# Row statistics, index casts and a weight load redistributed in the opening of a graph-convolution and expert kernel

## What is computed

```python
xn = layernorm(x)                                   # eps 1e-5
h  = ln_w * xn * rsqrt(mean(xn**2) + 1e-6)          # per row
out = h @ W_root + bias                             # 1024 -> 286
for r in range(2):                                  # edge types
    w = (edge_type == r)
    sums = segment_sum((h[src] @ W_rel[r]) * w, dst)
    out += sums / max(segment_sum(w, dst), 1)
x = x + xn + elu(out) @ wo                          # 286 -> 1024
xf = layernorm(x)
x = x + xf + mean(2 shared experts(xf)) + top-2 of 8 routed experts(xf)
```

## Time and profile before

| | us |
|---|---|
| median of 3 runs | 342.8 (342.51 to 343.4) |
| the profiled execution | 342.85 |
| its span in the trace | 341.1 |
| busy: PE | 318.1 (93%) |
| busy: DVE | 231.9 (68%) |
| busy: ACT | 160.2 (47%) |
| busy: POOL | 74.6 (22%) |
| last addition of the group loop ends | 76.95 |
| first matmul of the aggregation | 81.65 |

### The profile page before, as it was taken

The page is one execution under the profiler, slowest core; times in us unless marked ns, Lnnn a source line. Parts: engine busy times, 40 slices in busy tenths (PEclk is TensorE's granted clock), DMA queues, the critical chain, the costliest instruction groups (busy, mean ns, idle before and its releaser), DMA issues.

```text
span 341.1 us, 5804 instructions
## 1 busy us (share of the span) xinstructions
PE 318.1 (93%) x1904; PEld 275.4 (81%) x1904; DVE 231.9 (68%) x444; ACT 160.2 (47%) x261; POOL 74.6 (22%) x91
## 2 busy tenths in 40 slices
PE   0989899998999999989998999998999999999994
PEld 0889798777889888869997888887888888868873
DVE  3999999987557456852756668556456656581994
ACT  2774969995122313342248485545645545520000
POOL 5580510001010110110031234222123410004840
PEclk9899999999999999999999999999999999999998
DMA  8960004000001126397043394699789991224994
GB/s 252 327 186 1 1 18 152 2 3 14 2 1 63 61 97 209 127 302 308 3 131 116 125 307 187 229 358 333 271 290 304 352 378 76 99 87 165 306 339 169
DMA packets 26752, 57.58 MB, mean 169 GB/s; under 512 B 2701, under 2 KB 16281, under 8 KB 26724
## 3 DMA queue, kind: packets, MB, share of 16 engines
q1 hardware_dynamic: 20198, 33.89, 29.2%
q0 software_dynamic: 3888, 14.16, 12.5%
q10 hardware_dynamic: 2638, 9.17, 6.8%
HBM read 66.25 MB, written 14.03 MB: 235 GB/s over the span
## 4 chain that ended last, share of the span: by engine, by line
PE 67%; DVE 17%; issue 5%; DVEq 3%; ACT 3%; DMA 2%; POOL 0%; ACTq 0%; SPq 0%
PE ps L1371 34%; PE ps L1639 16%; PE ps L1485 5%; PE ps L1629 4%; DVE arena_r L510 3%; DVEq L1028 2%; DVE work L1014 2%; DVE st L950 2%; DVE big L1025 2%; DMA y_acc<-in_x 2%; DVE xt L958 1%; PE ps L1520 1%; PE ps L1448 1%; PE ps L1381 1%; PE ps L1647 1%
## 5 line engine op out<-in xcount | busy, mean ns | idle before, releaser
L1371 PE MATMUL ps<-arena_r 128*128 128x512 f32 (+1 forms) x264 | 67.3, 401 | 0.2 <-DVE arena_r L1101 0.2
L1639 PE MATMUL ps<-big,tile 128*128 x272 | 61.8, 380 | 2.0 <-ACT tile L872 1.0
L1371 PE MATMUL ps<-arena_r,xt 128*128 128x286 f32 (+1 forms) x360 | 60.0, 310 | 1.2 <-DVE arena_r L510 1.1
L1371 PE MATMUL ps<-xt,arena_r 128*128 128x314 f32 (+2 forms) x312 | 59.7, 343 | 0.2 <-DVE xt L1092 0.2
L1639 PEld LDWEIGHTS ps<-big,tile 128*128 128x128 f32 x272 | 51.4, 190 | 10.1 <-issue 2.6
L1371 PEld LDWEIGHTS ps<-arena_r 128*128 128x128 f32 (+1 forms) x264 | 48.0, 188 | 10.9 <-DVE arena_r L1101 0.6
L1371 PEld LDWEIGHTS ps<-xt,arena_r 128*128 128x128 f32 (+1 forms) x312 | 50.2, 187 | 6.5 <-DVE xt L1092 0.5
L619 POOL DMA_INDIRECT big<-xrow,tok_i x17 | 31.6, 1858 | 100.7 <-PE ps L1629 76.4
L1371 PEld LDWEIGHTS ps<-arena_r,xt 128*128 128x128 f32 (+1 forms) x360 | 50.7, 192 | 1.9 <-issue 1.3
L902 ACT ACTIVATE arena_r<-raw 128x2048 fp32r x17 | 32.5, 1910 | 27.8 <-DMA raw<-in_L_ffn_W 17.9
L1300 DVE TENSOR_TENSOR arena_r<-raw,arena_r 128x2048 fp32r<-128x2048 f32 x17 | 38.8, 2283 | 2.1 <-ACT arena_r L902 2.1
(11 more groups left out here) (213 smaller groups left out, 373.6 us busy)
## 6 DMA issues: line engine op xcount, KB each, us to landing
big<-in_L_ffn_W SPq DMA_DIRECT2D x19, 1024.0 KB, 7.5
raw<-in_L_ffn_W SPq DMA_DIRECT2D x19, 1024.0 KB, 10.3
yrow<-work ACTq DMA_DIRECT2D x17, 512.0 KB, 3.5
raw<-in_L_gnn_W_rel SPq DMA_DIRECT2D x2, 1144.0 KB, 11.7
y_acc<-in_x SPq DMA_DIRECT2D x4, 512.0 KB, 8.1
xrow<-work SPq DMA_DIRECT2D x4, 512.0 KB, 2.9
raw<-in_L_ffn_sW SPq DMA_DIRECT2D x2, 1024.0 KB, 5.9
sw_raw<-in_L_ffn_sW SPq DMA_DIRECT2D x2, 1024.0 KB, 12.6
```

The lines of the kernel that those rows point to most:

```text
L1371: ins = pe.matmul(out_ap, a, b, start=start and k == 0, stop=stop and k == n - 1)
L1639: ins = pe.matmul(ps[1][:, i % 2, 0:HID], xg_t[:, k * P:(k + 1) * P], big[:, bass.ds(ring * UNIT + k * HID, HID)], start=k == 0, stop=k == ...
```

## The change

- ScalarE takes the statistics of x tiles 2 to 4, in a new `stats_centre(t)`: an activation with an accumulated sum for the mean, the centring, and a square with an accumulated sum for the variance, with a small activation behind each sum for the division. `stats_x(2)`, `(3)` and `(4)` on VectorE go.
- GpSimd casts src and edge type to floats. TensorE transposes dst, src and edge type as they are; the shift and the two combinations are done by VectorE in `groups()` on the transposed 125x160 arrays. dst has a semaphore of its own.
- SyncE issues w_rel[1] ahead of x tiles 2 to 4.
- GpSimd clears the first half of `big`, waits for `groups()`, makes the first batch of row factors, and then clears the second half.
- `ACT_HOT` begins at group 11, `LO_AT` has three entries, and ScalarE's order is written anew; `weights_hi(2)` comes after split 3.

```diff
-        dst_f, lo_f, hr_f = (work[0:G, i * EG:(i + 1) * EG] for i in range(3))
-        hi_i = work[0:G, 3 * EG:4 * EG].bitcast(I32)
+        dst_f, src_f, rel_f = (work[0:G, i * EG:(i + 1) * EG] for i in range(3))
...
             load_rel(0)
+            load_rel(1)
             for t in range(2, T):
                 load_x(t)
-            load_rel(1)
...
+            pool.wait_ge(s_edge, 32)
+            pool.tensor_copy(src_f, src_i).then_inc(s_cast, 1)
+            pool.tensor_copy(rel_f, rel_i).then_inc(s_cast, 1)
             pool.wait_ge(s_kf, 1)
...
+            zero(0, NZ // 2)
+            pool.wait_ge(s_grp, 1)
...
             row_scales(slice(0, 3))
+            zero(NZ // 2, NZ)
             row_scales(slice(3, T))
...
-        LO_AT = {4: 3, 6: 2, 9: 8, 15: 3}
+        LO_AT = {6: 3, 9: 10, 15: 3}
...
-        ACT_HOT = tuple(range(7, G, 2))
+        ACT_HOT = tuple(range(11, G, 2))
...
-            for to, frm in ((dst_i, dst), (rel_i, rel), (src_i, src)):
-                act.dma_start(to, frm.rearrange("(p e) -> p e", e=EG)).then_inc(s_edge, 16)
+            for to, frm, done in ((dst_i, dst, s_dst), (src_i, src, s_edge), (rel_i, rel, s_edge)):
+                act.dma_start(to, frm.rearrange("(p e) -> p e", e=EG)).then_inc(done, 16)
...
+            def stats_centre(t):
+
+                r, row = rows[t], y_acc[0:rows[t], t, :]
+                junk = xn[(t + 1) % NXN][0:r, :]
+                act.wait_ge(s_x[t], 16 * len(row_parts(r)))
+                act.wait_ge(s_xr, t - 1)
+                act.activation(junk, row, ACT.Copy, accum_out=sums[0:r, 0, t:t + 1]).then_inc(s_sum, 1)
+                act.wait_ge(s_sum, 3 * t - 5)
+                act.activation(mv[0:r, t, 0:1], sums[0:r, 0, t:t + 1], ACT.Copy, scale=1.0 / D).then_inc(s_sum, 1)
+                act.wait_ge(s_sum, 3 * t - 4)
+                act.activation(xn[t % NXN][0:r, :], row, ACT.Identity,
+                               bias=mv[0:r, t, 0:1], scale=-1.0).then_inc(s_n, 1)
+                act.wait_ge(s_n, t + 1)
+                act.activation(junk, xn[t % NXN][0:r, :], ACT.Square, accum_out=sums[0:r, 1, t:t + 1]).then_inc(s_sum, 1)
+                act.wait_ge(s_sum, 3 * t - 3)
+                act.activation(mv[0:r, t, 1:2], sums[0:r, 1, t:t + 1], ACT.Copy, scale=1.0 / D).then_inc(s_mv, 1)
+                act.wait_ge(s_mv, t + 1)
...
             split_rows(1, 1)
-            weights_hi(1, 0, KD // 2)
-            centre(2)
-            weights_hi(1, KD // 2, KD)
+            stats_centre(2)
+            weights_hi(1)
             split_rows(2, 2)
-            weights_hi(2)
...
-            centre(3)
+            stats_centre(3)
             h_out(0)
+            stats_centre(4)
+            h_out(1)
             split_rows(3, 3)
+            weights_hi(2)
             act.wait_ge(s_grp, 1)
             act.activation(neg_lo, lo_t, ACT.Copy, scale=-1.0).then_inc(s_neg, 1)
             act.wait_ge(s_neg, 1)
-            h_out(1)
             src_distance(0)
-            centre(4)
-            act_hots(0, 3)
+            act_hots(0, 1)
             h_out(2)
-            act_hots(3, 4)
+            act_hots(1, 2)
             split_rows(4, 4)
-            act_hots(4, 7)
+            act_hots(2, 5)
             h_out(3)
-            act_hots(7, 15)
+            act_hots(5, 13)
             h_out(4)
-            act_hots(15, len(ACT_HOT) - 1)
+            act_hots(13, len(ACT_HOT) - 1)
...
-                v.mark(dve.tensor_copy(hr_t, hr_p))
+                step(dve.tensor_copy(hi_t, src_p))
+                step(dve.tensor_scalar(hi_t, hi_t, 7, None, ALU.arith_shift_right))
+                v.mark(dve.scalar_tensor_tensor(lo_t, hi_t, -float(P), src_p, ALU.mult, ALU.add))
+                v.mark(dve.scalar_tensor_tensor(hr_t, hi_t, float(R), rel_p, ALU.mult, ALU.add))
...
-                v.mark(dve.tensor_copy(lo_t, lo_p))
...
-            dve.wait_ge(s_edge, 48)
-            v.mark(dve.tensor_copy(dst_f, dst_i))
-            step(dve.tensor_scalar(hi_i, src_i, 7, None, ALU.arith_shift_right))
-            v.mark(dve.scalar_tensor_tensor(lo_f, hi_i, -float(P), src_i, ALU.mult, ALU.add))
-            v.mark(dve.scalar_tensor_tensor(hr_f, hi_i, float(R), rel_i, ALU.mult, ALU.add))
+            dve.wait_ge(s_dst, 16)
+            step(dve.tensor_copy(dst_f, dst_i))
...
-            stats_x(2)
             groups()
             weights_lo(dve, 1)
             split_rows_lo(2, 2)
-            stats_x(3)
...
-                    if at == 0:
-                        stats_x(4)
-                    elif at == 2:
+                    if at == 1:
                         weights_lo(dve, 2)
                     else:
-                        split_rows_lo(3 + at // 3, 3 + at // 3)
+                        split_rows_lo(3 + at // 2, 3 + at // 2)
...
-            for n, v in enumerate((dst_f, lo_f, hr_f)):
+            pe.wait_ge(s_cast, 2)
+            for n, v in enumerate((dst_f, src_f, rel_f)):
```

More of the change, by code:

```diff
@@ L185, in program @@
                                     for i in range(4))
+        hi_t = mid[0:CE, 4 * EC:5 * EC].bitcast(I32).rearrange("p (g c) -> p g c", c=CG)
         assert 5 * EC <= 3 * F
@@ L203, in program @@
         scale = sb("scale", [P, T])
+        sums = sb("sums", [P, 2, T])
         ends = sb("ends", [G, 2])
@@ L266, in program @@
         s_x = [sem(f"s_xin{t}") for t in range(T)]
+        s_dst = sem("s_dst")
         s_edge = sem("s_edge")
+        s_cast = sem("s_cast")
+        s_sum = sem("s_sums")
         s_convb = sem("s_convb")
@@ L559, in _, with zero @@
             cols = big.shape[1] // NZ
-            for i in range(NZ):
-                pool.memset(big[:, i * cols:(i + 1) * cols], 0.0).then_inc(s_az, 1)
             assert NZ * cols == big.shape[1]
+            def zero(first, last):
+                for i in range(first, last):
+                    pool.memset(big[:, i * cols:(i + 1) * cols], 0.0).then_inc(s_az, 1)
+            zero(0, NZ // 2)
+            pool.wait_ge(s_grp, 1)
             own = Tally(s_p)
@@ L965, in groups @@
                 parts = [ps[3][0:CE, 1, n * EC:(n + 1) * EC].rearrange("p (c g) -> p g c", c=CG) for n in range(3)]
-                dst_p, lo_p, hr_p = parts
+                dst_p, src_p, rel_p = parts
                 d0_v = d0_b[:, :].rearrange("p (g a) -> p g a", a=1).to_broadcast([CE, G, CG])
                 v.mark(dve.tensor_copy(d0_b[:, :], ps[2][0:CE, 1, 0:G]))
-                v.mark(dve.tensor_copy(hr_t, hr_p))
+                step(dve.tensor_copy(hi_t, src_p))
+                step(dve.tensor_scalar(hi_t, hi_t, 7, None, ALU.arith_shift_right))
+                v.mark(dve.scalar_tensor_tensor(lo_t, hi_t, -float(P), src_p, ALU.mult, ALU.add))
+                v.mark(dve.scalar_tensor_tensor(hr_t, hi_t, float(R), rel_p, ALU.mult, ALU.add))
                 step(dve.tensor_scalar(far_f[:, :], ps[2][0:1, 1, G:G + 2], 1.0, None, ALU.min))
```

## The result

| | before | after |
|---|---|---|
| median | 342.8 us | 341.28 us (340.77 to 341.86, 5 runs) |
| ratio of after to before | | 0.995, 95% interval 0.9933 to 0.9967 |
| the profiled execution | 342.85 us | 341.86 us |
| its span | 341.1 us | 340.1 us |
| busy: VectorE / ScalarE | 231.9 / 160.2 us | 226.7 / 165.2 us |

The change saves 1.5 us by the medians and 1.0 between the two profiled executions; 1.8 was forecast. The profiled execution of the changed kernel is the slowest of its five. The gain is there, but the path to it is not quite the one I drew.

A forecast was written before the change was run, and what follows sets the result against it. VectorE was taken to bound the kernel up to the end of the group loop. Group 6 comes 2.45 us earlier, less 0.7 for two returned tables: 1.8 us gained, 342.85 - 1.8 = 341.0 us, range 339.1 to 342.9.

The forecast's parts named there:

- Statistics on ScalarE, 4.1 us a tile: ScalarE's queue, x tiles 2 to 4: sums, read-outs, small activations and centring 3.95 us, about 4.1 with hand-overs.
- Rival (b): ScalarE's six accumulated sums ahead of split 3 are dear; at 0.75 each 1.5 us slower, 344.4 us; chance 0.12.
- (a): ScalarE quicker than charged: read-outs hidden (-1.15), x tile 2 there when ScalarE is free (-0.75); 339.1 us; chance 0.14.
- x tile 2 at 16.2: Load stream: with w_rel[1] ahead, x tile 2 lands at 16.2 us (15.5 to 17.2); ScalarE starts at 16.3.
- Casts by 11 us: GpSimd's casts of src and rel, 1 us each, done by 11 us, under the transposes of x tile 1.
- rival (c): GpSimd's casts are late: at 2.85 us each they end at 14.65, 1.65 us lost, 342.7 us; chance 0.10.
- groups() 0.7 longer: VectorE's index arithmetic in groups() on 125x160: two more and longer instructions, +0.7 us (bounds 0.4 and 1.2).
- VectorE waits some 2.3 us at split 3, group 6 at 36.35: VectorE, at split 3 by 32.9, waits 2.3 us for ScalarE and starts group 6's tables at 36.35, not 38.82.
- rival (d): Gain doesn't reach the loop's end: x tile 2 lands at 17.2, later part has 0.8 us less in hand; 342.4; chance 0.10.
- end by 22.36 + 1.03 = 23.4 at the latest: TensorE's transposes of tile 2 end by 23.4 us, before ScalarE reaches split 2 at 23.8, so no wait.
- theory Q: Experiments' theory: ScalarE's queue, with its split 2 wait for TensorE's tile 2 transposes beyond 23.1 us, sets group 6.

The follow-up runs named there:

- the third: Third trace of the changed kernel, from a repeat with no edit, against the kernel before: ratio 0.9931 (0.9906 to 0.9956).
- the index part alone: Kernel before with only GpSimd's casts of src and edge type, shift and combinations in groups(), and a semaphore for dst: ratio 0.9955 (0.9936 to 0.9973).
- the second and third: Traces from two repeats of the changed kernel with no edit, against the kernel before: ratios 0.9947 and 0.9931.

## Why the prediction was right, and where it was off

The forecast was 341.0 us in a range of 339.1 to 342.9; the median is 341.28.

*Statistics on ScalarE, 4.1 us a tile*: 4.02, 4.01 and 4.00, from the start of each to what follows. The accumulated sum costs 0.06 us more in the pass and 0.19 for the read-out. Rival (b) falls, and (a) in its first half; its second half, tile 2 there when ScalarE is free, came nearly true: a wait of 0.28 us in the first trace and none in the third.

*x tile 2 at 16.2*: ScalarE starts it at 15.84. The second matrix, issued at 2.2, landed 12.2 later, at 14.4; it took 3.4 us of the stream and not the 3.8 that I charged.

*Casts by 11 us*: two of 0.59, from 7.61 to 8.75; rival (c) falls. They cost nothing.

```profile
7.61 0.59 POOL L540 CAST work<-sw_raw 40x500 f32<-40x500 int32 x1 [2.23 <-DMA sw_raw<-in_edge_type]
```

*groups() 0.7 longer*: wrong in sign. 3.83 us (16.85 to 20.68) against 4.2. I knew the 0.96 us compare, and charged the new instructions without taking back in the sum what the collision with GpSimd had cost; the same compare takes 0.24 now.

*VectorE waits some 2.3 us at split 3, group 6 at 36.35*: 2.33 us and 35.46 where TensorE is fast; 1.62 us and 37.65 in the first trace. From there to the last addition both take 38.80 us, 0.67 more than before, as charged; the loop gives nothing back otherwise, so rival (d) falls too.

*The step that failed* is the sentence that the transposes of tile 2 "end by 22.36 + 1.03 = 23.4 at the latest". I took a time of the kernel before as a bound for the new one. TensorE's speed in the opening differs from run to run: in the three traces of the changed kernel they ended between 21.3 and 25.2. Split 2 had 0.4 us of room over those 23.4 in my drawing and none in fact, as ScalarE was there by 22.9 to 23.4; so this time became a second term of the sum, +0 to +2, which I had put at nothing. It cancelled with the 0.9 us by which the queue itself was quicker. So the size 1.8 (measured 1.5) is right in part by luck: the single traces gave 0.5, 2.7 and 2.9 at the last addition, against the one trace of the kernel before.

*What brought the gain*: I put it down to the whole change through ScalarE's queue. The runs say that the index part alone gives 1.3 us in the kernel before, by VectorE's path, while the rest of the change alone (statistics, loads, clearing and lists together) measures 0.999. That moving the statistics in this order adds little fits the wait at split 3: the work taken off VectorE (4.4 us) stands again in front of it. With the statistics of tile 4 behind split 3 the kernel is 0.5 to 0.7% faster. How the gain splits between the parts inside the changed kernel stays open, as the run without the index part has more loss than theory Q gives it.

## What to carry to other kernels

Work moved off the bounding engine brings only what the new owner can do before the old one asks for it: write out the new queue up to the first hand-over, and put moved work behind that hand-over where nobody needs it sooner. A time of another engine in the old trace is a bound for the new one only if that engine is not itself near the path; where it had a wait to spare before, look how far it varies. And moved work changes what it runs beside: in the kernel before with the index part the instructions taken away in front gave 1.0 us (groups() starts at 18.63 instead of 19.63), and one compare that no longer ran beside GpSimd's clearing gave 0.7.

## What the runs showed of the hardware

- An activation with an accumulated sum is two rows: the pass (1024 elements, 1.04 to 1.06 us against 1.00 plain from PSUM) and ACTIVATION_READ_ACCUMULATOR (0.18 to 0.20 us).
- GpSimd's cast of 500 int32 per partition to floats took 0.59 us, near its memset (0.97 for 1075 elements) and far from its iota (2.28 for 400).
- In the opening TensorE's matmuls of 286 columns took 441 ns in slow stretches and about 295 otherwise. In the first trace of the changed kernel it was slow from its first matmul at 7.9 until 20.6 us; in the second and third the first transposes were slow (1.94 us for eight) and the 48 matmuls hardly at all (6.92 and 7.04 us, against 6.74 with no slow stretch in them in the kernel before with the index part). Slow stretches came also after 8 us of steady matmuls. The granted clock's record showed some of them at 0.50 (the kernel before, 16 to 18 us) and read 1.00 over others. Eight transposes took 1.94 us after idling and 1.04 after matmuls.
- From the last addition to the end of the span the traces took 262.8 to 264.9 us, in no order that follows the variants: 2 us of scatter that no change here explains, more than the change itself saves. A single trace's total time is no measure of the change; its last addition is a better one.
